# Record scatters issued in twos: GpSimd waits for all earlier ones to land before every third, fifth and seventh of a group

## What is computed

```python
h = tok(x, w1, b1, w2, b2)                                   # [16, 128, 256]
h = h + attn(layernorm(h), Wq, Wk, Wv, Wo, rel_emb)          # 16 heads of 16
g = softmax(x @ Wg + bg); keep the top 2 of 8, divide by their sum
eo = gelu(x @ W1[e] + b1[e]) @ W2[e] + b2[e]                 # 256 -> 1024 -> 256
h = h + sum over the two experts of g * eo                   # x = layernorm(h)
```

## Time and profile before

| what | value |
|---|---|
| median of 3 runs | 585.12 us (585.07 to 585.44) |
| the profiled execution | 583.82 us |
| its span | 582.0 us |
| TensorE matmul | 521.7 us busy, 90% |
| weight load beside it | 427.2 us, 73% |
| ScalarE | 267.6 us, 46% |
| VectorE | 235.3 us, 40% |
| GpSimd | 200.6 us, 34% |
| DMA | 78.55 MB, 135 GB/s over the span |
| record scatters (L433) | 32, mean 980 ns on GpSimd |

### The profile page before, as it was taken

The page is one execution under the profiler, slowest core; times in us unless marked ns, Lnnn a source line. Parts: engine busy times, 40 slices in busy tenths (PEclk is TensorE's granted clock), DMA queues, the critical chain, the costliest instruction groups (busy, mean ns, idle before and its releaser), DMA issues.

```text
span 582.0 us, 13228 instructions
## 1 busy us (share of the span) xinstructions
PE 521.7 (90%) x3742; PEld 427.2 (73%) x3743; DVE 235.3 (40%) x1083; ACT 267.6 (46%) x1003; POOL 200.6 (34%) x186
## 2 busy tenths in 40 slices
PE   4799889899889988986899999999999999999990
PEld 3466555566556655644899989999999999999970
DVE  2677677777658756644112411111111111111110
ACT  1267677778667766844334332333333333333310
POOL 3132133224443344361133355333333333333221
PEclk9899999999889988985999999999999999999995
DMA  8890020212030303037556565666666666666614
GB/s 264 270 294 2 19 92 20 93 36 92 2 91 18 91 19 92 18 102 255 169 150 170 160 173 176 182 181 182 180 181 181 181 180 181 181 181 182 180 25 153
DMA packets 50999, 78.55 MB, mean 135 GB/s; under 512 B 10528, under 2 KB 39472, under 8 KB 50768
## 3 DMA queue, kind: packets, MB, share of 16 engines
q1 hardware_dynamic: 40160, 66.80, 35.5%
q0 software_dynamic: 8592, 10.58, 10.8%
q10 hardware_dynamic: 2208, 0.71, 0.6%
HBM read 68.27 MB, written 11.90 MB: 138 GB/s over the span
## 4 chain that ended last, share of the span: by engine, by line
PE 50%; issue 28%; POOL 9%; DMA 4%; DVE 3%; another core or an unknown queue 2%; ACT 2%; POOLq 0%; SPq 0%; DVEq 0%; ACTq 0%
PE psVO L972 21%; PE psS L960 12%; PE psP L960 11%; POOL kbd L259 4%; DMA fold<-xn_dram,sel 2%; POOL rstd L424 2%; POOL meta_dram L433 2%; PE psQK L790 2%; PE psQK L948 2%; ACT prob L587 1%; DMA sel<-meta_dram 1%; PE psP L823 1%; DVE prob L1138 1%; DMA sum_dram<-fold,sel 1%
## 5 line engine op out<-in xcount | busy, mean ns | idle before, releaser
L972 PE MATMUL psVO<-xw,prob 128*128 x624 | 141.6, 380 | 0.8 <-DVE fold L1359 0.8
L972 PEld LDWEIGHTS psVO<-xw,prob 128*128 128x128 f32 x624 | 115.6, 190 | 15.5 <-issue 1.2
L487 POOL DMA_INDIRECT sum_dram<-fold,sel x39 | 61.7, 1582 | 167.3 <-DMA sel<-meta_dram 123.5
L587 ACT ACTIVATE prob<-prob,smin 128x128 f32<-128x128 f32 x256 | 99.5, 394 | 10.4 <-DVE smin L1138 8.1
L680 ACT ACTIVATE prob<-psS,b1T 128x128 f32<-128x128 f32 x160 | 45.5, 368 | 98.1 <-PE psS L960 93.0
L424 POOL TENSOR_TENSOR rstd<-ve,minus_half 128x1 f32<-128x1 f32 x32 | 29.0, 906 | 165.1 <-DVE ve L1101 165.1
L680 ACT ACTIVATE prob<-psP,b1T 128x128 f32<-128x128 f32 x152 | 43.2, 373 | 85.5 <-PE psP L960 81.6
L960 PEld LDWEIGHTS psS<-fold,w1c 128*128 128x128 f32 x640 | 77.0, 198 | 1.9 <-DVE fold L1354 1.0
L960 PE MATMUL psS<-fold,w1c 128*128 128x128 f32 x640 | 77.6, 281 | 0.6 <-DVE fold L1354 0.6
L960 PEld LDWEIGHTS psP<-fold,w1c 128*128 128x128 f32 x608 | 70.7, 192 | 3.0 <-DVE fold L1354 2.1
L960 PE MATMUL psP<-fold,w1c 128*128 128x128 f32 x608 | 71.1, 275 | 1.9 <-DVE fold L1354 1.9
(11 more groups left out here) (165 smaller groups left out, 542.9 us busy)
## 6 DMA issues: line engine op xcount, KB each, us to landing
w1c<-in_L_ffn_W SPq DMA_DIRECT2D x39, 1024.0 KB
xw<-in_x SPq DMA_DIRECT2D x16, 512.0 KB, 7.2
xw<-in_L_ffn_W SPq DMA_DIRECT2D x8, 1024.0 KB
sum_dram<-h_all SPq DMA_DIRECT2D x17, 128.0 KB
xn_dram<-xn SPq DMA_DIRECT2D x16, 128.0 KB
out<-sum_dram SPq DMA_DIRECT2D x4, 512.0 KB, 5.7
relb<-in_L_ffn_b SPq DMA_DIRECT2D x1, 1024.0 KB, 4.7
sel<-meta_dram SPq DMA_DIRECT2D x39, 2.0 KB
```

The source lines that it names most:

```text
L487: pool.indirect_dma_start(out=sum_dram.ap()[0:EARLY_B * S if j < EARLY else N_TOK + P, :], out_offset=bass.IndirectOffsetOnAxis(ap=row_no[ ...
L587: i = act.activation(blk, blk, ACT.Exp, bias=smin[:, k:k + 1], scale=-1.0, accum_out=ssum[:, k:k + 1])
L972: i = pe.matmul(psVO[:, 0:D], hT[u][:, c * P:(c + 1) * P], xw2[:, bass.ds(e * (HC * D) + c * D, D)], start=(c == 0), stop=(c == HC - 1))
```

## The change

In `scatter_records` GpSimd now waits, before each scatter whose running number i over the whole kernel is even (and not 0), until all i scatters before it have landed (16 counts each). A group starts at a multiple of 8, so its first, third, fifth and seventh scatter have such a wait.

```diff
                 for i in range(g * NG * TOPK + a, g * NG * TOPK + b):
+                    if i >= 2 and i % 2 == 0:
+                        pool.wait_ge(scat, 16 * i)
                     pool.indirect_dma_start(
                         out=meta_dram.ap()[:, :],
```

## The result

The changed kernel took 579.23 us (median of 4 runs, 577.93 to 580.53), the kernel before on the same chip 585.28 us (585.07 to 586.6): ratio 0.9884, 95% interval 0.9853 to 0.9915. It is 6 us faster where 6 us slower was forecast. The profiled execution took 578.61 us, its span 576.6 us; before 583.82 and 582.0.

The account below looks back on a forecast made before the run. TensorE was taken as the bound, the expert stage having no room for a later start. Group of eight +6.0, groups 0 and 1 0, group 3 +0.3 gave +6.3: 585.12 + 6.3 = 591.4 us, range 587.5 to 596.

Parts of the forecast that it names:

- the term of groups 0 and 1: Waits in each half of four scatters there: covered by 4.7 us before GpSimd's next work, so cost nothing.
- the clock at tile 0: Rival: tile 0's matmuls take 3.84 not 6.50 us as the clock returns earlier; 582.8 us in all; chance 0.05.
- The sum at the group of eight: Group 2's waits, scatter by scatter, put tile 0's records at 271.6 for 265.58: +6.0 us, ends +5.1 and +9.2.
- The hold-up behind W2: Group 2's second scatter stands behind a 1 MB W2 block, out at 258.4 not 253.4; the third waits for it.
- the rival of prompt landing: Group 2's scatters each land in 1.8 us: +1.0 or less, 585.5 to 586.1 us; chance 0.10 together with no effect.
- the slack of 3.6 us: Hand-over to experts: scatter packets started by 261.0, tile table written until 264.6, so 3.6 us of waiting is free.
- Caught twice: Rival: group 2's fourth scatter falls behind b2 as the second does behind W2: +9.2, 594.6 us; chance 0.13.
- Group 3: Waits before scatters in the expert stage delay a few gathers behind W1 blocks: +0.3 us, ends 0 and 1.5.
- The clock: TensorE's half clock around tile 0 moves along with tile 0; otherwise up to 2.7 us less or more.
- The sign: Whole kernel: the change makes it slower, chance 0.88, against same 0.08 and faster 0.04.

Follow-up runs that it names:

- e1_g01: Kernel before plus the waits in groups 0 and 1 alone, chip 9: 569.82 us, ratio 1.0005 to the kernel before.
- e11_g01: Kernel before plus the waits in groups 0 and 1 alone, repeated on chip 4: 571.06 us, ratio 0.9772 to the kernel before.
- e6_after: The changed kernel run again unchanged, on chip 6: 578.13 us, ratio 1.0137 to the kernel before.
- e2_g2: Kernel before plus the waits in group 2 alone, chip 9: 578.59 us, ratio 1.0152 to the kernel before.
- e8_w2early: Changed kernel with the last W2 block issued one image earlier, chip 6: 572.91 us, ratio 1.0048 to the kernel before.
- e18_pauses_only: Kernel before plus six short GpSimd pauses (one power each) among the scatters of groups 0 to 2, no waits, chip 14: 572.25 us, ratio 0.9766.
- e17_pauses: Kernel before plus six one-power GpSimd pauses in groups 0 to 2, last W2 block earlier, b2 behind the second W1 block, chip 14: 570.39 us, ratio 0.9731.
- e7_g3: Kernel before plus the waits in group 3 alone, chip 6: 570.73 us, ratio 1.0003 to the kernel before.
- e13_after: The changed kernel run again unchanged, on chip 0: 576.87 us, ratio 0.9849 to the kernel before.
- e15_short: Kernel before plus one GpSimd power between second and third scatter of each half in groups 0 and 1, no waits, chip 0: 570.47 us, ratio 0.9738.

## Why the prediction was wrong

**What failed** is one step: the term of groups 0 and 1, "cost nothing", put at 0 in the sum. As a cost it was right: where there is no stall the waits there cost nothing (`e1_g01` on chip 9, the same within 0.3%). But I priced the waits only against the idle time behind them, never asked why that idle time was there, nor read who waited for what while the four scatters ran. So a gain was ruled out: the range of this term was closed at zero from below, on no row. The term is -14.2 us in the first trace (first scatter of group 2 at 250.22, then 236.37, with the stage's start 0.33 later), and `e11_g01` alone shows it: -13.9. No rival had it either; the one on the side of faster, the clock at tile 0, is another mechanism, and had 0.05.

**The sum at the group of eight** was right on the critical terms. Third scatter 10.1 us after the first (forecast 9.2: 7.73 us idle, 7.00 in `e6_after` and 8.10 in `e2_g2`), eighth 18.6 (18.7), records +6.4 (+6.0). `e2_g2` has +8.3 for it in the kernel's time, `e6_after` +7.3. The hold-up behind W2, weighed against the rival of prompt landing, stood the test of `e8_w2early`. One part of its working doesn't carry over: the slack of 3.6 us. The tile table was last at 264.6 because DVE itself was stalled in group 2 (1.87, 2.56 and 0.53 us by "remote" between 254 and 261 us); in the changed kernel it is ready 8.8 us after the first scatter and no longer 14.2. Yet `e1_g01` on chip 9, with no stall, has its records 14.9 us after the first scatter, and the stalled kernel before 15.4: there the last of eight unwaited scatters starts at 8.9 us, and SP goes on 6.0 later, against 3.1 in the changed kernel. Without the stall b2 comes earlier and holds them: in `e1_g01` it is issued at 242.69, and the last 96 packets of q0 are started only between 248.0 and 249.5; on chip 14 SP goes on 6.7 us after the last scatter's start in `e18_pauses_only`, and 3.15 us, as in the changed kernel, in `e17_pauses`, where b2 and the W2 block are out of the way. So the slack was there in the trace that I priced from, but as a product of the stall; that two different waits put the records at 15.4 and 14.9 us, and the +6.0 so near to the +6.4, is luck. (A slip beside it: by the sum the first turn would come at 272.45 + 6.0 = 278.5, not 278.7.)

**Caught twice** did not happen: b2 was issued at 242.64, 6.3 us after the group's first scatter where the forecast kept 11.2 (261.44 - 250.22), and so ahead of the third scatter and not at the fourth. **Group 3**: forecast +0.3; `e7_g3` alone is the same as before within 0.25%. The 2.12 us at 355.88 are no wait at a scatter (GpSimd has its usual gap there), but a gather that lands late at another time against the W1 blocks; `e6_after` has 0.47 at that place. **The clock** at tile 0: its matmuls took 5.69 us for 6.50, a gain of 0.8 within the bounds of 2.7; more of it, by the rows at 150 to 170 us, was in the attention stage, where I hadn't looked.

**The sign.** With no stall to remove the forecast's side was right (`e6_after` on chip 6, and `e2_g2` on chip 9); on the chip where it was made and on chip 0 (`e13_after`) it wasn't; on 8, 4 and 14, which have the stalls too, the changed kernel was not run. The near hit on chip 6, +7.3 for +6.3, is of the terms at the group of eight, and says nothing for the forecast where it was made. The trace of before was of the stalled kind and showed it: 10.4 us of waits on ScalarE, beside 7.6 on DVE, for results of TensorE that were long written, at exactly the bursts that the change breaks up.

**What stays open.** Which part of the chip holds back the signals, why only on some chips or at some times, whether the sender or the receiver is held, and whether the pace of issue counts or what is still under way: no run here looks inside. That GpSimd's run of indirect DMAs sets it off is shown by `e11_g01` to `e15_short`: waits at two places and pauses of two lengths, which share only that no four go out in a row, all end the stalls in groups 0 and 1 (in group 2 shorter runs only shorten them, `e17_pauses`); that it is TensorE's signals alone is only what the named waits are.

## What to carry to other kernels

Before pricing an edit at an instruction, list the waits at that time on the engines that it doesn't touch, and compare each with the end of what it waits for: a releaser "remote" or "unknown" on one core, with the producer long done, is time that an edit can free. Break a burst of GpSimd's indirect DMAs by some other work of its own rather than by waiting for their landing, which cost 7 to 8 us here where a megabyte stood in the queues. And run a change of a few per cent on more than one chip: here the same edit was 1.2% faster on one and 1.4% slower on another.

## What the hardware did that was not expected

- Four record scatters of 128 rows in a row, starts 1.26 to 1.43 us apart, held other engines back by up to 2.6 us, until 0.9 us after the last; with 0.78 us between the middle two (one small power of GpSimd), not at all in groups 0 and 1.
- That happened on chips 8, 4, 0 and 14 and in the first comparison, and on chips 6 and 9 not at all, with the same program: 583 to 586 us and 570 to 571 us. Each was used in one sitting.
- A scatter of 128 records, 2 KB in all, stood behind a 1 MB transfer of another queue, so that the next one waited 6.8 to 8.1 us for its landing (`e13_after`, `e6_after`, the first trace, `e2_g2`); with that block moved 1.8 us (`e8_w2early`). In groups 0 and 1, beside stores and other blocks of W2, such waits were 1.4 to 6.0 us.
